# Eight value products in a row: pairing the sets of layers 0 and 3 on TensorE

## What is computed

```python
# layer 0: 16 heads of width 16, 512 queries and 512 keys per batch entry
attn = softmax(einsum('bhqd,bhdk->bhqk', q * scale, k))
mean = einsum('bhqk,bhkd->bhqd', attn, v)
ex2  = einsum('bhqk,bhkd->bhqd', attn, v * v)
std  = sqrt(relu(ex2 - mean * mean))
out  = instance_norm(x) * std + mean
# layer 3: 16 heads of width 16, 512 queries and 512 keys per batch entry
ctx  = einsum('bhqk,bhkd->bhqd', softmax(einsum('bhqd,bhkd->bhqk', Q, K) / 4), V)
r    = ctx @ Wo + q
out  = gelu(layer_norm(r) @ W1 + b1) @ W2 + b2 + r
```

## Time and profile before

| | us |
|---|---|
| median of 3 runs | 3052.73 |
| lowest and highest run | 3046.79, 3060.24 |
| span of the profiled execution, first to last instruction | 3046.7 |
| PE busy, of the span | 2781.9 (91%) |
| DVE / ACT / POOL busy, of the span | 1739.8 / 1353.9 / 1006.5 |

### The profile page before, as it was taken

How to read it: one execution, slowest core, us unless ns; L and a number is a source line. 1 busy time by engine, 2 the same in 40 slices (tenths; PEclk the granted TensorE clock), 3 DMA queues, 4 the chain that set the end, 5 groups by cost and what they waited for, 6 DMA issues and landing times.

```text
span 3046.7 us, 41581 instructions
## 1 busy us (share of the span) xinstructions
PE 2781.9 (91%) x14752; PEld 1327.7 (44%) x14752; DVE 1739.8 (57%) x4302; ACT 1353.9 (44%) x2383; POOL 1006.5 (33%) x846
## 2 busy tenths in 40 slices
PE   5998899989999999999999999998878899898997
PEld 2322222235555555556665566553432333333333
DVE  5777777734443333311457655766567767677661
ACT  1666666653333333331333443343314555555563
POOL 1777777763443444420000100011221322332110
PEclk7999999999999999899999999998888999999998
DMA  5444444321002001202333323333342332233220
GB/s 123 101 107 102 106 105 102 85 88 58 18 27 82 29 30 36 70 25 89 58 63 68 71 68 63 72 67 75 70 115 78 76 92 70 76 90 86 63 54 28
DMA packets 182463, 219.94 MB, mean 72 GB/s; under 512 B 40968, under 2 KB 135792, under 8 KB 176112
## 3 DMA queue, kind: packets, MB, share of 16 engines
q1 hardware_dynamic: 170192, 189.74, 26.9%
q0 software_dynamic: 6016, 20.98, 2.0%
q10 hardware_dynamic: 6048, 6.56, 0.7%
HBM read 146.90 MB, written 51.64 MB: 65 GB/s over the span
## 4 chain that ended last, share of the span: by engine, by line
PE 57%; DVE 11%; DMA 10%; SPq 7%; issue 5%; POOL 5%; ACT 4%; ACTq 0%; DVEq 0%; POOLq 0%
PE PS L594 23%; PE PS L846 7%; SPq L1748 3%; PE PS L983 2%; DVE l_M L1492 2%; DMA l_RB<-l_recs 2%; PE PS L765 2%; PE PS L915 2%; PE PS L963 2%; PE PS L973 2%; PE PS L881 2%; PE PS L787 2%; PE PS L723 2%; PE PS L1016 2%; POOL l1a_S L1611 2%
## 5 line engine op out<-in xcount | busy, mean ns | idle before, releaser
L1273 DVE TENSOR_REDUCE l_M<-PS 128x1 f32<-128x512 f32 x512 | 329.6, 682 | 113.0 <-PE PS L704 112.9
L1492 DVE TENSOR_REDUCE l_M<-PS 128x1 f32<-128x512 f32 x512 | 332.2, 683 | 93.2 <-PE PS L963 89.3
L1576 POOL TENSOR_TENSOR l_S<-l_P 128x512 f32<-128x512 f32 x256 | 327.9, 1313 | 79.6 <-ACT l_P L1054 79.6
L1211 ACT ACTIVATE l_P<-PS 128x512 f32<-128x512 f32 x512 | 279.5, 600 | 161.6 <-PE PS L973 142.5
L1054 ACT ACTIVATE l_P<-PS 128x512 f32<-128x512 f32 x512 | 282.5, 597 | 124.5 <-PE PS L713 123.4
L1332 DVE TENSOR_REDUCE l1a_M<-PS 128x1 f32<-128x512 f32 x256 | 158.8, 683 | 241.2 <-PE PS L768 241.2
L1400 DVE CUSTOM_DVE_ANT_0 l_JK<-PS,l_MK 128x256 f32<-128x256 f32 x512 | 195.7, 419 | 133.6 <-PE PS L881 130.0
L963 PE MATMUL PS<-l_KS,l_QS 97*128 97x512 bf16 x512 | 200.7, 403 | 45.8 <-DVE l_M L1492 42.3
L594 PE MATMUL PS<-l_YT,l_w_mlp_w 128*128 128x256 f32 x1024 | 233.2, 384 | 3.4 <-ACT l_YT L1132 2.6
L846 PE MATMUL PS<-l_w_mlp_w,l_H 128*128 128x512 f32 x512 | 230.4, 597 | 3.2 <-ACT l1a_P L1107 2.3
L704 PE MATMUL PS<-l_KS,l_QS 97*128 97x512 bf16 x512 | 197.9, 403 | 37.7 <-DVE l_M L1273 25.1
(11 more groups left out here) (249 smaller groups left out, 4732.8 us busy)
## 6 DMA issues: line engine op xcount, KB each, us to landing
l_QS<-q_scratch SPq DMA_DIRECT2D x128, 128.0 KB, 5.5
q_scratch<-l_T SPq DMA_DIRECT2D x96, 128.0 KB
k_scratch<-l_T SPq DMA_DIRECT2D x96, 128.0 KB
l_QS<-q_scratch SPq DMA_DIRECT2D x32, 384.0 KB, 4.9
l_KS<-k_scratch SPq DMA_DIRECT2D x32, 384.0 KB
l_QS<-q_scratch SPq DMA_DIRECT2D x32, 256.0 KB, 5.5
l_KS<-k_scratch SPq DMA_DIRECT2D x32, 256.0 KB
l_RB<-l_recs SPq DMA_DIRECT2D x32, 256.0 KB
```

The lines of the kernel that those rows point to most:

```text
L1211: e.activation(t.P[quad % 4][:, m, :], PS[:, COUNTS.bank[st], :], ACT.Exp, scale=0.25).then_inc(q.sem("act.exp", st), 1)
L1273: e.tensor_reduce(t.M[i % 2][:, qt, hd:hd + 1], PS[:, COUNTS.bank[st], :], AX.X, ALU.max).then_inc(q.sem("dve.smax", st), 1)
L1492: e.tensor_reduce(t.M[i % 2][:, qt, hd:hd + 1], PS[:, COUNTS.bank[st], :], AX.X, ALU.max).then_inc(q.sem("dve.smax", st), 1)
L1576: x = e.tensor_tensor(t.S[j % 2][:, m, :], t.P[2 * j % 4][:, m, :], t.P[(2 * j + 1) % 4][:, m, :], ALU.add)
```

## The change

In the lists of steps of layers 0 and 3, `vals` with an even number is placed right before its odd neighbour: the place n/8 becomes (n + 1 - n % 2)/8, with 0.0001 n to keep the two in order. Sets 0, 2, 4 and 6 of each item thus stand an eighth of an item later; sets 1, 3, 5 and 7 stay. No instruction is added or dropped, and the sizes are the same. A new function `late` reads a further table, `MOVED`, which is empty, so it gives what `LATER` gave.

```diff
 def layer0_order():
...
         out = [(0.25 + (j + 0.4) / 32, k("sc", j)) for j in range(32)]
         for n in range(8):
-            out.append((0.425 + n / 8, k("vals", n)))
+            out.append((0.425 + (n + 1 - n % 2) / 8 + 0.0001 * n, k("vals", n)))
...
 def layer3_order():
...
-        out += [(3.25 + (j + 0.4) / 32, k("sc", j)) for j in range(32)] + [(3.45 + n / 8, k("vals", n)) for n in range(8)]
+        out += [(3.25 + (j + 0.4) / 32, k("sc", j)) for j in range(32)] + [(3.45 + (n + 1 - n % 2) / 8 + 0.0001 * n, k("vals", n)) for n in range(8)]
...
+MOVED = {
+}
+
+def late(st, engine):
+
+    moved = MOVED.get((st[0], st[3]), MOVED.get((st[0], -1), {}))
+    return LATER.get((st[0], engine), 0.0) + moved.get(engine, 0.0)
```

More of the change, by code:

```diff
@@ L201, in order_of @@
     for part in parts:
-        late = sorted((at + LATER.get((st[0], engine), 0.0), n, st) for n, (at, st) in enumerate(part[:-1]))
-        out += [st for _, _, st in late] + [st for _, st in part[-1:]]
+        late_at = sorted((at + late(st, engine), n, st) for n, (at, st) in enumerate(part[:-1]))
+        out += [st for _, _, st in late_at] + [st for _, st in part[-1:]]
     return out
```

## The result

The changed kernel takes 3072.72 us (median of 5 runs, 3067.59 to 3082.13) against 3052.88 us for the kernel before (3046.79 to 3061.68) on the same chip: ratio 1.0068, 95% interval 1.0046 to 1.0089. It is slower by about 20 us. The forecast was 3047 us with a range to 3070; both the sign and the range were missed, the range by 3 us.

The account below looks back on a forecast made before the run. TensorE was taken as the fullest engine but not the only bound. Terms of -9.4, -15.3 and +15.5 gave -9.2 us; 3.4 for the clock made -6, so 3047 us against the median, range 3027 to 3070.

Parts of the forecast that it names:

- The price of a boundary: On TensorE, entering and leaving a lone vals set costs 0.09 + 0.14 = 0.23 us; 128 boundaries go, 29.4 us.
- rival 5: The fixed price comes with each vals set whatever stands beside it, so only moves count: +4.4, 3057 us; chance 0.05.
- The four buffers of P: Exponentials of set 2k + 4 need set 2k's buffer; cover shrinks from 0.34 to 0.21 of an item, costed at nothing.
- The two dangerous places: Layer 0, set 6 ahead of the maxima's DMAs and set 0 ahead of ACT's square roots: even sets leave the waits' shadow.
- Starving the others: During a pair DVE and ACT get no new bank; up to 0.7 us a pair, set at nothing, bound 11 us.
- Only the odd one on it: 18 pairs in layers 0 and 3 whose even set leaves the shadow of a wait: 18 x 0.86 = 15.5 us lost.
- Rival 2: Sets leave the shadows of waits everywhere: 38.7 us lost against 19.1 gained, +19.6, 3072 us; chance 0.17.
- Both on the chain: 41 pairs in layers 0 and 3 with both sets on the chain save a boundary: 41 x 0.23 = 9.4 us gained.
- only the even one: 14 pairs in layers 0 and 3 whose even set moves behind where the path leaves TensorE: 14 x 1.09 = 15.3 us gained.
- The clock: Two further half-speed stretches of TensorE behind longer waits, 1.7 us each: 3.4 us lost, from a possible 0 to 27.

Follow-up runs that it names:

- experiment 5: Layer 0 only, against the kernel before: sets 0 and 6 moved next to 1 and 7 with one smax, or one sc, left between: 1.0046 and 1.0045.
- l0_six: Against the kernel before, only set 6 of each item in layer 0 moved behind to pair with set 7: 3069.35 us, 1.0056.
- l0_56: Against the kernel before, only set 5 of each item in layer 0 moved behind to pair with set 6: 3055.28 us, 0.9998.
- near_outer: Against the kernel before, sets 0 and 6 of layer 0 moved later but kept one sc and one smax from 1 and 7, unpaired: 3054.78 us, 0.9993.
- l0_outer: Against the kernel before, only the outer pairs of layer 0 (sets 0+1 and 6+7) made: 3080.03 us, 1.0109.
- l3_pairs: Against the kernel before, all pairs in layer 3 alone, layer 0 as before: 3050.99 us, 1.0008.
- l3_but0: Against the kernel before, layer 3 only, all pairs but that of set 0 in the second item of each two: 3052.60 us, 1.0000.
- chosen: As l3_but0, with set 4 of each second item in layer 0 paired too, against the kernel before: 3048.45 us, 0.9999.
- l0_pairs: Against the kernel before, all pairs in layer 0 alone, layer 3 as before: 3071.21 us, 1.0076.
- l0_odd: Against the kernel before, sets 1+2 and 5+6 paired in layer 0 only: 3052.94 us, 1.0003.
- l0_inner: Against the kernel before, only sets 2+3 and 4+5 paired, in layer 0 alone: 3054.39 us, 1.0022.
- both_odd: Against the kernel before, sets 1+2 and 5+6 paired in layers 0 and 3: 3058.62 us, 1.0017.

## Why the prediction was wrong, point by point

**Right.** The price of a boundary: a pair lasts 1.86 us at full clock, as forecast, so rival 5 (it doesn't do what it says) is out. The four buffers of P were cover enough: in the changed kernel's trace no exponential waits for a `vals` set. The two dangerous places, sets 6 and 0 of layer 0, were named, and the loss is there.

**The step that failed: "Starving the others".** It was set at nothing, with 11 us as the bound for the range, and the loss came through it: some 20 us. Three things were wrong in it. It reckoned a pair at full clock only, 2.40 us from `smax` to `smax`; behind a wait the pair often runs at half speed, and then it is 3.86 us. It looked at DVE alone; experiment 5 shows that a bank for ACT in the middle of the pair is worth as much as one for DVE. And it took as cover that DVE has work of its own where it is late, and that both engines even out over a pair where TensorE is late; but DVE's wait for `smax` rose by 48.6 us, and TensorE's wait for DVE rose as well. What is dear is a run of two sets right behind a wait: TensorE is often at 1.2 GHz there, the engines it should feed have just come free, and they get nothing for up to 3.6 us. l0_six against l0_56 shows the place, near_outer against l0_outer the length. The rate: the outer pairs cost 33 us and saved 32 x 0.23 = 7, so some 40 us gross in 32 pairs, 1.25 us each, where the step allowed 0.7 in 16 places.

**"Only the odd one on it", 15.5 us lost: wrong for the kernel's time.** The price was for leaving the shadow, and near_outer, which leaves it without pairing, costs between -6 and +2 us; only the 8.2 us at its layer 0's end, in one execution, speak for a price. Rival 2 (sets fall out of the shadows everywhere) gave 3072 us, the measured time, by this same reason; its number was met by chance, not by its mechanism. It counted 45 waits at 0.86 us each, but in the trace of the kernel before only 21 of the waits at these places are that long, and l0_six against l0_56 and near_outer against l0_outer show a loss that needs the pair. The wait for the DMAs, which that mechanism would have raised, fell from 15.6 to 5.6 us.

**"Both on the chain" and "only the even one", 24.7 us gained: wrong.** l3_pairs should have gained 11 us and gained nothing measurable; l3_but0 and chosen should have gained 16 and 21. A chain of waits says what came last in one execution. It doesn't say how close behind the next thing was, and here it was close: in layer 3 the waits for DVE and ACT grew by 12 us where TensorE was spared 10.

**The clock: mis-sized.** 3.4 us were taken; from the windows it is up to about 12 us in the middle of layer 0, with the clock at 0.93. How much of that reached the time isn't shown, since near_outer (also 0.93, 190.6 ns per product) isn't slower on the whole. The untouched layers 1 and 2 change the loss by some us from trace to trace, and not one way: up to the first `sc` of layer 3 it goes from 23.4 to 20.5 us in the changed kernel, but from 23.5 to 26.9 in l0_pairs, which has the same order up to there.

**Left open.** How the gross loss of a badly placed pair splits between half speed and the empty banks. Near_outer against l0_outer is waiting, net of the saved boundaries, l0_six against l0_56 nearly all speed, and no run kept TensorE at full clock behind a wait. Why the 6 of 64 pairs that are slow in layer 3, behind waits too, leave no loss there. And why nothing is gained by pairs at full clock: l0_odd saves 32 boundaries, 7 us, and shows +1, with an interval of -4 to +6, where a saving of a half and none can't be told apart; l0_inner and both_odd even come out 7 and 5 us slower, with all but 1 of 32 and 2 of 64 pairs at full clock, by intervals that just leave out zero.

## What to carry to other kernels

Merging short bursts of one engine into longer ones saves its switching cost, but the others are fed in lumps; look first at what stands right ahead of the merged burst. In these traces TensorE is often slow behind a wait, just when everything else has run empty, and there small pieces in turn are worth more than saved switches. And a count of steps on the chain of one execution is no estimate of a gain when other engines show waits of the same size next to it.

## What the runs showed of the hardware

- Products close behind a wait, as the 1.73 us shown above, often run at 1.2 GHz in these traces (16 of the 25 pairs so placed in layer 0 of the changed kernel, none of the 39 others): a pair then takes up to 3.58 us instead of 1.86.
- A boundary between full-width products and products in strips of 32 columns costs a lone set 0.14 us behind it, also with 512 columns (two lone sets 2 x 1.00, a pair 1.86), plus 0.09 us ahead of it.
- A row maximum over 256 of 512 columns took 419 ns against 682, so by a straight line through these two (an estimate) 0.16 us of it don't depend on the columns. Cutting it in layers 0 and 3 moved the whole kernel by 1.3%, 39 us: the largest effect in this study.
